# Row norms between the softmax sums, a reordered prologue, and keys, values and router norms moved ahead, in an eight-stage transformer kernel on one core

## The chip, the cores and the metric

The kernel runs on one core of a Trainium2 chip. The core has five engines with a queue of instructions each: TensorE (PE, with its weight loads shown as PEld), VectorE (DVE), ScalarE (ACT), GpSimd (POOL) and SyncE (SP, which here only issues transfers). They meet only through semaphores. The metric is the time of one execution on the device in microseconds (us); lower is better.

## The reference, cut to what matters

The input x is 16 batches of 128 tokens of width 128; the context is 16 x 77 tokens of the same width. Four layers follow, each with an attention-like part and an FFN-like part, and each part is added to x with the tanh of a gate:

```
x = x + tanh(g_xattn[0]) * L0_xattn(layernorm(x), ctx, ctx, mask)  # 16 heads of 64, masked, softmax
x = x + tanh(g_ffn[0])   * L0_ffn(layernorm(x))     # switch MoE, 8 experts, capacity S/E
x = x + tanh(g_xattn[1]) * L1_xattn(layernorm(x), ctx)  # linear mix, plus the mean of ctx
x = x + tanh(g_ffn[1])   * L1_ffn(layernorm(x))     # SwiGLU, fake-quantised by global maxima
x = x + tanh(g_xattn[2]) * L2_xattn(layernorm(x), ctx, ctx)  # one head of 128
x = x + tanh(g_ffn[2])   * L2_ffn(layernorm(x))     # top 2 of 8 experts, and 2 shared ones
x = x + tanh(g_xattn[3]) * L3_xattn(layernorm(x), ctx)  # self and context attention, 16 heads of 8
x = x + tanh(g_ffn[3])   * L3_ffn(layernorm(x))     # expert choice over tokens
```

`layernorm` is (x - mean) / sqrt(var + eps) over the 128 features, without weights. In `L0_xattn` q = x wq + bq and k = ctx wk + bk. In `L2_ffn` the gates are a softmax over the two highest router logits of each token.

## The kernel before

x stays on the chip as tile `X` [128 tokens, 16 batches, 128]. Each stage has one function for each engine (`tensor_attn0`, `vector_attn0`, `scalar_attn0`, `gpsimd_attn0` and so on), and each engine runs the stages one after the other, in the order in which the code is written. So the order of work in a queue is the order by hand; `wait_ge(semaphore, n)` holds an engine until another has counted up to n. `linked` and `pooled` make an engine wait for its own last result. A float32 product is run by PE in two passes, so that the trace counts two for each instruction. Timeline rows join neighbours of one line, as x4.

**First attention** (`*_attn0`, 0 to about 250 us). In the prologue wq and wk are multiplied into a key weight per head (`G0`; L622), and wq with bk into `beta` (L628: 16 products, each of 64 rows, since two heads share the 128 partitions), wv and wo into a value weight (`wvo0`; L645), and bv and wo into a bias row (L649, L650). DVE and ACT copy them out of the PSUM banks, `prep0_*` being the semaphores. Then comes a loop over the 16 batches. For each one PE makes keys (L516) from ctx and `G0`, scores (L546 adds the mask, L547 multiplies), transposes of the exponentials (L559), values (L525, L534) and the output (L591). DVE takes maxima (L723, L727), subtracts (L732), sums the exponentials in three pieces (`sums`, L738, each after ACT's exponential of that piece, L901), and inverts the sums (L741); POOL multiplies by them (L1006). Rows of batch b+2 are normalised in turn b: DVE's `stats` (L706, L708), POOL's rstd (L990, L991), DVE's `apply` (L713, tile `xn`), PE's transpose (L575), ACT's copy (L906). DVE also normalises rows for the first router within the loop.

**First MoE and linear mix** (250 to 345 us). Tokens go to experts by indirect transfers through memory and come back the same way (`y_tokens`); DVE adds the returned ones to X (L1301). The mix (`tensor_mix1`) has a product that spreads per-batch rows (L1273), six warming products on ones (`keep_busy`, L445), and then for four groups of four batches: transposes (L1253), ACT's copy, product.

**Quantised FFN** (345 to 385 us). At its end DVE has, for each of four groups, an output scaling and an addition to X (L1443, L1445).

**Third attention** (`*_attn2`, 385 to 427 us). First keys and values of all 16 batches (L1478: three products, L1482: sixteen), copied by ACT (L1562) and DVE (L1524, with the bias) into `kT2` and `v2` in area A of the on-chip memory. Then four groups: the norm of the rows in DVE (`vector_g_stats`, L1229, L1232; `vector_g_apply`, L1246) and POOL (L1237, L1238), transposes (L1253), queries (L1493), scores (L1498), maximum and subtraction (L1531, L1533), exponential (L1573), transposes (L1511), product with values (L1517), scaling and addition (L1555, L1557).

**Second top-2 MoE** (`*_moe2`, 427 to about 540 us). For each of the four groups: statistics, rstd and rows, transposes into bank `GT2`, ACT's copy into `xnT2` (L1747), logits (L1609). Then DVE's `route` (L1684 to L1700): top two, differences, an exponential by ACT (L1751), gates, and their split into bfloat16 parts (L1697 to L1700). PE meanwhile does `up(0)` and `up(1)` (L1616) and the context keys and values of the fourth attention (`tensor_aux3`: L1831, L1835; ACT L2049, L2053). POOL's `gpsimd_aux3` (L2119 to L2122) splits these keys into bfloat16 parts, which SP sends on (`sync_aux3`). Then PE transposes the gates (L1622), and pairs of experts run: `up` (L1616), ACT's Silu (L1743), DVE's products (L1712, L1714). ACT loads a table of functions when it goes from Exp to Silu or back (ACT_TABLE_LOAD rows).

## Time and profile before

| | |
|---|---|
| median of three runs | 797.06 us |
| the runs | 792.36, 797.06, 799.18 us |
| the profiled execution | 798.87 us, span 796.5 us |
| mean granted clock of TensorE | 0.884 |
| PE busy | 629.6 us (79%) |
| DVE busy | 455.9 us (57%) |
| ACT busy | 325.3 us (41%) |
| POOL busy | 216.0 us (27%) |
| busy PE, 46 to 250 us | 189.22 of 204 us |
| busy PE, 385 to 430 and 430 to 475 us | 32.47 of 45 and 35.34 of 45 us |

The span is what the profiler recorded from the first to the last instruction; the time of the execution has a little more around it. The granted clock is the share of full speed that the throttle let TensorE have; its levels are 2.4 GHz (1.00) and 1.2 GHz. A row of the timeline has start, duration, engine, line, operation, output<-inputs, shapes; in brackets how long the engine was idle before it and what released it. Engines work side by side, so only the one that others wait for sets the time.

### The profile page before, as it was taken

How to read it: one execution, taken by the hardware profiler on the slowest of the kernel's cores; microseconds unless marked ns; L12 is line 12 of the kernel's file. 1: busy time of each engine (PE TensorE's matmuls, PEld its weight loads, DVE VectorE, ACT ScalarE, POOL GpSimd, SP SyncE). 2: the span in 40 equal slices, each digit the busy share in tenths (PEclk: the TensorE clock that was granted, in tenths of full speed). 3: DMA queues.
4: the chain of work that ended last, by engine and by line, in shares of the span. 5: the costliest groups of instructions: out<-in, count | busy, mean ns of one | idle time of the engine just before them, and what ended most of it. 6: DMA issues, size and time to landing. Idle time of an engine off the chain costs nothing.

```text
span 796.5 us, 14168 instructions
## 1 busy us (share of the span) xinstructions
PE 629.6 (79%) x5413; PEld 420.5 (53%) x5413; DVE 455.9 (57%) x1244; ACT 325.3 (41%) x700; POOL 216.0 (27%) x407
## 2 busy tenths in 40 slices
PE   3889999999988596553685879989888878857687
PEld 3656565666656384421454525554555555534674
DVE  2266576676767412779666455536666666165362
ACT  1354435353433241534231422313676676512154
POOL 2032323334253446400112212421252511020210
PEclk9999999999999698656797779999899999755789
DMA  7840000000000253000000040203020300020001
GB/s 241 226 163 1 1 1 1 1 7 8 1 9 19 90 159 112 0 0 1 1 0 1 0 109 15 78 7 103 5 77 21 91 7 6 3 107 0 2 0 54
DMA packets 33604, 34.50 MB, mean 43 GB/s; under 512 B 8730, under 2 KB 29506, under 8 KB 32962
## 3 DMA queue, kind: packets, MB, share of 16 engines
q1 hardware_dynamic: 31072, 31.02, 13.4%
q0 software_dynamic: 1024, 2.11, 0.8%
q8 instruction: 44, 0.72, 0.4%
q10 hardware_dynamic: 1442, 0.48, 0.3%
q14 instruction: 22, 0.18, 0.1%
HBM read 19.62 MB, written 5.26 MB: 31 GB/s over the span
## 4 chain that ended last, share of the span: by engine, by line
PE 51%; DVE 18%; issue 12%; ACT 11%; POOL 4%; DMA 1%; POOLq 0%; DVEq 0%; ACTq 0%; SPq 0%
PE bank L1616 5%; PE bank L1859 5%; PE bank L591 4%; PE bank L547 4%; PE bank L1874 3%; ACT area_a L927 3%; PE bank L1661 3%; PE bank L1907 2%; ACT area_a L901 2%; PE bank L525 2%; PE bank L2287 2%; PE bank L534 2%; POOL y_tokens L1197 2%; DVE mx L2010 2%; ACT area_a L920 2%
## 5 line engine op out<-in xcount | busy, mean ns | idle before, releaser
L2010 DVE TENSOR_REDUCE mx<-bank 128x4 f32<-128x512 f32 (+1 forms) x128 | 71.0, 581 | 39.7 <-PE bank L1867 39.3
L2078 ACT ACTIVATE area_a<-bank 128x512 f32<-128x512 f32 (+1 forms) x128 | 73.7, 597 | 39.2 <-PE bank L1874 37.8
L927 ACT ACTIVATE area_a<-bank,beta 128x154 f32<-128x154 f32 x128 | 42.0, 413 | 85.9 <-PE bank L516 85.8
L591 PEld LDWEIGHTS bank<-area_a 128*128 128x128 f32 x384 | 46.7, 191 | 24.7 <-issue 24.7
L1006 POOL TENSOR_TENSOR area_a<-area_a,rs 128x512 f32<-128x512 f32 (+1 forms) x48 | 40.9, 879 | 60.6 <-DVE rs L741 60.6
L591 PE MATMUL bank<-area_a 128*128 128x128 f32 x384 | 53.5, 283 | 0.0
L746 DVE COPY area_a<-bank 128x512 f32<-128x512 f32 x32 | 22.1, 689 | 42.1 <-PE bank L525 21.1
L1237 POOL TENSOR_TENSOR g_veps<-g_mv,eps 128x4 f32<-128x4 f32 x20 | 4.0, 201 | 152.5 <-DVE g_mv L1232 152.5
L1616 PE MATMUL bank<-area_a 128*128 128x512 f32 x80 | 43.1, 668 | 0.2 <-DVE area_a L1714 0.2
L516 PE MATMUL bank<-ctx_flat,area_a 128*128 128x154 f32 x256 | 41.4, 296 | 2.3 <-ACT area_a L927 2.2
L516 PEld LDWEIGHTS bank<-ctx_flat,area_a 128*128 128x128 f32 x256 | 36.3, 190 | 10.3 <-issue 7.1
L547 PE MATMUL bank<-area_a,xnT 128*128 128x512 f32 (+1 forms) x96 | 41.6, 515 | 0.0
L1253 PE MATMUL bank<-ident,xn 128*128 128x128 f32 x80 | 17.8, 364 | 26.2 <-DVE xn L1246 15.8
L525 PE MATMUL bank<-area_a,ctx_flat 128*64 128x512 f32 x128 | 34.3, 617 | 0.1
L920 ACT ACTIVATE area_a<-bank 128x512 f32<-128x512 f32 x48 | 29.9, 624 | 8.7 <-PE bank L559 8.7
L445 PE MATMUL bank<-ones_b 128*128 128x512 bf16 x84 | 25.8, 415 | 7.6 <-DVE drow L1102 5.3
L990 POOL TENSOR_TENSOR ln_veps<-ln_mv,eps 128x1 f32<-128x1 f32 x32 | 6.3, 196 | 92.2 <-DVE ln_mv L708 90.8
L901 ACT ACTIVATE area_a<-area_a 128x512 f32<-128x512 f32 (+1 forms) x48 | 28.3, 590 | 6.6 <-DVE area_a L732 6.6
L2159 POOL CAST mcol<-mx 128x16 bf16<-128x16 f32 x32 | 5.3, 196 | 93.3 <-DVE mx L2010 93.3
L559 PE MATMUL bank<-ident,area_a 128*128 128x128 f32 x192 | 29.2, 277 | 1.7 <-ACT area_a L920 1.7
L559 PEld LDWEIGHTS bank<-ident,area_a 128*128 128x128 f32 x192 | 22.3, 141 | 15.1 <-issue 15.1
L1874 PE MATMUL bank<-area_a,area_b 64*77 64x128 bf16 x256 | 23.3, 231 | 8.6 <-ACT area_a L2078 8.0
(360 smaller groups left out, 1513.8 us busy)
## 6 DMA issues: line engine op xcount, KB each, us to landing
area_a<-xn_area SPq DMA_DIRECT2D x48, 128.0 KB, 2.7
area_b<-in_w SPq DMA_DIRECT2D x16, 256.0 KB, 4.9
f<-in_f SPq DMA_DIRECT2D x1, 2048.0 KB
area_a<-in_f SPq DMA_DIRECT2D x1, 2048.0 KB, 7.9
area_b<-xn_area SPq DMA_DIRECT2D x6, 308.0 KB, 5.6
area_a<-in_rows SPq DMA_DIRECT2D x10, 128.0 KB, 2.7
x_slots<-xn_area SPq DMA_DIRECT2D x1, 1032.0 KB, 7.4
area_a<-x_slots SPq DMA_DIRECT2D x8, 129.0 KB, 2.4
```

The source lines that it names most:

```text
L516: m = pe.matmul(dst[:, (h - lo) * 2 * T:(h - lo + 1) * 2 * T], G0[:, h, :], ctx_flat[:, 2 * g * T:(2 * g + 2) * T], start=True, stop=True)
L525: m = pe.matmul(dst[64 * r:64 * r + 64, :], ctx_flat[:, b * T:b * T + 64], wvo0[:, 8 * n + r:8 * n + 8:2, :], start=True, stop=True)
L547: pe.matmul(S0[c][:, 0:n * w], xnT[:, b % 2, :], kk0[:, b // 2 % 2, lo:hi, (b % 2) * T + t0:(b % 2) * T + t1], start=False, stop=True).the ...
L559: m = pe.transpose(T0[c % 2][:, i * 128:(i + 1) * 128], flat(part), ident[:, :])
L591: m = pe.matmul(WO, eT0[:, i, :], vv0[:, b % 2, i, :], start=(i == 0), stop=(i == 11))
L901: act.activation(probs0(b, c), probs0(b, c), ACT.Exp, scale=DK0 ** -0.5).then_inc(exp_done, 1)
L920: act.activation(flat(eT0[:, 4 * c:4 * c + 4, :]), T0[c % 2][:, :], ACT.Copy).then_inc(turn_done, 1)
L927: m = act.activation(kk0[:, g % 2, h, :], src[:, (h - lo) * 2 * T:(h - lo + 1) * 2 * T], ACT.Identity, bias=beta0[:, h:h + 1])
L1616: m = pe.matmul(SETS2[n % 2][a][:, :], w13_2[:, a, PAIRS2[n % 5], :], xnT2[:, n // 5, :], start=True, stop=True)
L1874: return pe.matmul(EXP_RING3[j % 2][0:n, i * 128:(i + 1) * 128], keys3(b, aux, p, ROWS3, c), queries3(b, p, ROWS3, c), start=True, stop=True)
L2010: dve.tensor_reduce(mx3[:, b % 2, aux, heads3(half, 1 - odd)], SCORES_RING3[j % 2][:, 0:4 * n].rearrange("p (h k) -> p h k", k=n), AX.X, A ...
L2078: act.activation((ea3 if aux else em3)[:, heads3(half, odd), :], EXP_RING3[j % 2][0:T if aux else 128, :].rearrange("p (h q) -> p h q", q= ...
```

## The change

1. In the loop of the first attention, `apply(b + 2)` (new line L720) goes from behind the reciprocal to between the first and the second of the three sums.
2. In the prologue, `bk0` is laid out as blocks [128, 8, 2], so that beta takes eight products of 128 rows. PE's order becomes: key weights, beta, transposes, keys 0 and 1, first value product, keys 2 to 5, scores, keys 6, second value product, keys 7, bias row, keys 8. DVE and ACT follow it. ident and ones are counted with the first rows of x; spare_slot goes behind the mask and ident_b in ACT's queue; POOL converts the mask behind the two rstd; the tanh goes behind the keys.
3. Keys and values of the third attention (`tensor_keys2` and its partners) go ahead of the mix; `kT2` and `v2` lie in area B. The six warming products go.
4. At the end of the quantised FFN, DVE does the statistics of all four groups of the third attention's norm, and the rows of the first two, between and behind its outputs.
5. In the third attention's loop, DVE and POOL do the router's norm for each group, and PE transposes groups 0 and 1 and makes their logits. Groups 2 and 3 follow in the second MoE.
6. In the second MoE, PE does `up(0)`, `up(1)` and two pieces of the fourth attention's context keys ahead of groups 2 and 3. ACT does keys, copies, two pieces of values, the exponential, the rest of the values and then the first Silu. POOL's split waits for the gates (`gates2_done`), and SP's transfers of constants for the end of the third attention.

```diff
-        bk0 = sb("bk0", [128, 8])
+        bk0 = sb("bk0", [128, 8, 2])
...
-        kT2 = carve("A", (at2, (B, T,)), 128)
-        v2 = carve("A", (at2, (B, D,)), T)
+        at2b = [0]
+        kT2 = carve("B", (at2b, (B, T,)), 128)
+        v2 = carve("B", (at2b, (B, D,)), T)
...
-                for r in range(2):
-                    p = slice(64 * r, 64 * r + 64)
-                    m = pe.matmul(bank[4 + r][:, j:j + 1], wq0[p, j, :], bk0[p, j:j + 1], start=True, stop=True)
+                m = pe.matmul(bank[4][:, 2 * j:2 * j + 2], wq0[:, j, :], bk0[:, j, :], start=True, stop=True)
             m.then_inc(prep0_in_psum, 1)
-            pe.wait_ge(const_loaded, 5 * 16)
+            pe.wait_ge(x_first, 3 * 16)
             for b in range(2):
                 pe.wait_ge(xn_done, b + 1)
                 pe.transpose(bank[6][:, b * 128:(b + 1) * 128], xn[:, b, :], ident[:, :]).then_inc(xnT_in_psum, 1)
-            pe.wait_ge(wvo0_loaded, 4 * 16)
...
-            pe.wait_ge(const_loaded, 5 * 16)
+            pe.wait_ge(x_first, 3 * 16)
...
+            pe.wait_ge(ctx_loaded, 16)
+            pe.wait_ge(prep0_act_done, 2)
+            pe.wait_ge(prep0_dve_done, 2)
+            keys(0)
+            keys(1)
+            value_weights(0)
+            for n in range(2, 6):
+                keys(n)
+            pe.wait_ge(prep0_dve_done, 4)
+            pe.wait_ge(pool_ready, 3)
+            pe.wait_ge(const_loaded, 3 * 16)
+            scores(0)
+            keys(6)
+            value_weights(1)
+            keys(7)
             for j in range(8):
                 pe.matmul(bank[7][0:1, 0:D], bv0[:, j:j + 1], wo0[:, j, :], start=(j == 0), stop=False)
             pe.matmul(bank[7][0:1, 0:D], ones_row[:, 0:1], bo0[:, :], start=False, stop=True).then_inc(prep0_in_psum, 1)
-            pe.wait_ge(ctx_loaded, 16)
-            pe.wait_ge(prep0_act_done, 2)
-            pe.wait_ge(prep0_dve_done, 4)
-            for n in range(6):
-                keys(n)
-            pe.wait_ge(pool_ready, 3)
-            scores(0)
-            for n in range(6, 9):
-                keys(n)
+            keys(8)
...
-            def sums(b):
+            def sums(b, norm=None):
+
                 u = b % 2
                 for c, (lo, hi) in enumerate(HEADS0):
+                    if c == 1 and norm is not None:
+                        apply(norm)
                     dve.wait_ge(exp_done, 3 * b + c + 1)
                     m = dve.tensor_reduce((slong0[:, lo:hi], slong0[:, lo:hi], sshort0[:, :])[c], probs0(b, c), AX.X, ALU.add)
...
+            key_weights(0)
             apply(0)
             apply(1)
-            dve.wait_ge(const_loaded, 5 * 16)
+            key_weights(1)
+            dve.wait_ge(prep0_in_psum, 3)
+            dve.tensor_copy(beta0[:, :], bank[4][:, 0:H0]).then_inc(prep0_dve_done, 2)
+            value_weights(0)
+            dve.wait_ge(const_loaded, 3 * 16)
             dve.wait_ge(pool_ready, 2)
             dve.tensor_copy(row_ids, spare_slot[:, :]).then_inc(ids_written, 1)
-            for half in range(2):
-                dve.wait_ge(prep0_in_psum, half + 1)
-                dve.tensor_copy(G0[:, 8 * half + 1:8 * half + 8:2, :], bank[2 * half + 1][:, :].rearrange("p (j d) -> p j d", d=D)).then_inc(prep0_dve_done, 1)
-            dve.wait_ge(prep0_in_psum, 3)
-            dve.tensor_copy(beta0[:, 0:H0:2], bank[4][:, 0:8])
-            dve.tensor_copy(beta0[:, 1:H0:2], bank[5][:, 0:8]).then_inc(prep0_dve_done, 2)
-            for half in range(2):
-                dve.wait_ge(prep0_in_psum, half + 4)
-                dve.tensor_copy(wvo0[:, 8 * half + 1:8 * half + 8:2, :], bank[5][:, :].rearrange("p (j d) -> p j d", d=D)).then_inc(prep0_dve_done, 1)
+            softmax(0)
+            value_weights(1)
+            sums(0)
...
-                    sums(j)
-                if b + 2 < B:
-                    apply(b + 2)
+                    sums(j, b + 2 if b + 2 < B else None)
...
+        def tensor_keys2(pe):
+            pe.wait_ge(late_loaded, LATE_LOADS * 16)
+            for n, (lo, hi) in enumerate(KB2):
+                if n == 2:
+                    pe.wait_ge(y_done, E0 - 1)
+                pe.matmul(KV2[n][:, 0:(hi - lo) * T], wqkv2[:, 1, :], ctxT[:, lo:hi, :].rearrange("p b t -> p (b t)"),
+                          start=True, stop=True).then_inc(kv2_in_psum, 1)
+            pe.wait_ge(y_done, E0)
+            for n in range(4):
+                at_least(pe, k2_done, n)
+                for j in range(4):
+                    m = pe.matmul(KV2[3 + n][0:T, j * D:(j + 1) * D], ctxT[:, 4 * n + j, :], wqkv2[:, 2, :], start=True, stop=True)
+                m.then_inc(kv2_in_psum, 1)
...
-            pe.wait_ge(y_done, E0)
+            tensor_keys2(pe)
             pe.wait_ge(mix16_done, 2)
             for g in range(4):
                 pe.matmul(MIX[g][:, :], ones[0:B, :], mix_rows[:, 4 * g:4 * g + 4, :].rearrange("p b d -> p (b d)"), start=True, stop=False)
-            keep_busy(pe, XT4[0], 6)
+            pe.wait_ge(v2_done, 3)
             tensor_g_xnT(pe, 0, XT4[0])
             for g in range(4):
+                if g == 0:
+                    pe.wait_ge(v2_done, 4)
...
+            vector_values2(dve)
...
+                if g < 2:
+                    vector_g_stats(dve, g, 8 + g, 3 * B + 4 * g + 4)
+                if g in (1, 2):
+                    vector_g_apply(dve, g - 1, 3 + g, 7 + g)
+            for g in range(2, 4):
+                vector_g_stats(dve, g, 8 + g, 3 * B + 4 * g + 4)
...
+            keep_busy(pe, bank[7], 6)
             tensor_g_xnT(pe, 4, XT4[0])
-            pe.wait_ge(v2_done, 4)
-            pe.wait_ge(k2_done, 3)
-            keep_busy(pe, AV2, 8)
+            pe.wait_ge(x_updated, 3 * B + 12)
+            keep_busy(pe, S2[0], 2)
...
+                else:
+                    tensor_g_xnT(pe, g + 6, GT2)
...
+                if g == 2:
+                    pe.wait_ge(moe2_loaded, 5 * 16)
+                if g >= 2:
+                    tensor_logits2(pe, g - 2)
...
+                if g >= 1:
+                    vector_g_stats(dve, g - 1, g + 11, 4 * B + 4 * g)
                 dve.wait_ge(av2_in_psum, g + 1)
                 out = tmp512[:, g % 2, :].rearrange("p (j d) -> p j d", d=D)
                 linked(dve, dve.tensor_tensor(out, AV2[:, :].rearrange("p (j d) -> p j d", d=D),
                                        s2["out"][:, :].unsqueeze(2).to_broadcast([128, 4, D]), ALU.mult))
                 dve.tensor_tensor(X[:, 4 * g:4 * g + 4, :], out, X[:, 4 * g:4 * g + 4, :], ALU.add).then_inc(x_updated, 4)
+                if g == 3:
+                    vector_g_stats(dve, 3, 15, 5 * B)
+                if g >= 1:
+                    vector_g_apply(dve, g - 1, g + 7, g + 11)
+            vector_g_apply(dve, 3, 11, 15)
...
-            for k in range(8, 12):
+            for k in range(8, 16):
...
-            tensor_aux3(pe)
+            pe.wait_ge(late_loaded, LATE_LOADS * 16)
+            pe.wait_ge(ahead_step, 7)
+            tensor_keys3(pe, 0)
+            tensor_keys3(pe, 1)
+            for g in range(2, 4):
+                tensor_g_xnT(pe, g + 8, GT2)
+                tensor_logits2(pe, g)
+            tensor_keys3(pe, 2)
+            for n in range(4):
+                tensor_values3(pe, n)
...
+            scalar_keys3(act, 0)
+            scalar_keys3(act, 1)
+            scalar_g_xnT2(act, 2)
+            scalar_g_xnT2(act, 3)
+            scalar_keys3(act, 2)
+            act.wait_ge(pool3_done, 1)
+            scalar_values3(act, 0)
+            scalar_values3(act, 1)
+            act.wait_ge(gap2_done, 1)
+            act.activation(r2s["e"][:, :], r2s["d"][:, :], ACT.Exp).then_inc(gap2_done, 1)
+            scalar_values3(act, 2)
+            scalar_values3(act, 3)
             silu(0, 0)
             silu(0, 1)
-            act.wait_ge(gap2_done, 1)
-            act.activation(r2s["e"][:, :], r2s["d"][:, :], ACT.Exp).then_inc(gap2_done, 1)
-            scalar_aux3(act)
...
-            for k in range(12, 16):
-                gpsimd_g_rstd(pool, k)
+            pool.wait_ge(gates2_done, 1)
             gpsimd_aux3(pool)
...
+            sp.wait_ge(x_updated, 5 * B)
...
+            act.dma_start(ident[:, :], t["ident"]).then_inc(x_first, 16)
+            act.dma_start(ones[:, :], t["ones"]).then_inc(x_first, 16)
             act.dma_start(mask_u8[:, :, :], t["mask"]).then_inc(mask_loaded, 16)
             act.dma_start(ident_b[:, :], t["ident_b"]).then_inc(const_loaded, 16)
+            act.dma_start(spare_slot[:, :], t["spare_slot"]).then_inc(const_loaded, 16)
```

PE in the prologue, before; area_a holds the weights, and L645 is the value product:

```order
L622 MATMUL bank<-area_a 128x128 x16
L628 MATMUL bank<-bk,area_a 128x1 x16
L633 MATMUL bank<-ident,xn 128x128 x2
L645 MATMUL bank<-area_a 128x128 x16
L649 MATMUL bank<-area_a,bv 1x128 x8
L650 MATMUL bank<-bo,ones 1x128
L516 MATMUL bank<-ctx_flat,area_a 128x154 x16
L546 MATMUL bank<-mask_bias,ident_b 128x208
```

And in the changed kernel:

```order
L638 MATMUL bank<-area_a 128x128 x16
L642 MATMUL bank<-bk,area_a 128x2 x8
L647 MATMUL bank<-ident,xn 128x128 x2
L517 MATMUL bank<-ctx_flat,area_a 128x154 x6
L628 MATMUL bank<-area_a 128x128 x8
L517 MATMUL bank<-ctx_flat,area_a 128x154 x10
L547 MATMUL bank<-mask_bias,ident_b 128x208
L517 MATMUL bank<-ctx_flat,area_a 128x154 x3
L628 MATMUL bank<-area_a 128x128 x8
```

The value product (now L628) stands between pieces of keys (L517), and the bias row (L649, L650 before) is behind the first scores.

DVE in the first full turn of the loop, before, with `xn` the rows of batch b+2:

```order
L706 BN_STATS ln_stats<-X 128x6
L708 BN_AGGR ln_mv<-ln_stats 128x2
L738 TENSOR_REDUCE slong<-area_a 128x8 x2
L738 TENSOR_REDUCE sshort<-area_a 128x16
L740 TENSOR_TENSOR sum<-slong,sshort 128x16
L741 RECIPROCAL rs<-sum 128x16
L713 TENSOR_SCALAR xn<-X,ln_mv,ln_rstd 128x128
L746 COPY area_a<-bank 128x512 x2
```

In the changed kernel:

```order
L713 BN_STATS ln_stats<-X 128x6
L715 BN_AGGR ln_mv<-ln_stats 128x2
L748 TENSOR_REDUCE slong<-area_a 128x8
L720 TENSOR_SCALAR xn<-X,ln_mv,ln_rstd 128x128
L748 TENSOR_REDUCE slong<-area_a 128x8
L748 TENSOR_REDUCE sshort<-area_a 128x16
L750 TENSOR_TENSOR sum<-slong,sshort 128x16
L751 RECIPROCAL rs<-sum 128x16
L756 COPY area_a<-bank 128x512 x2
```

The row of `xn` has moved up past two sums, the addition of the sums and the reciprocal.

PE at the start of the second MoE, before. The first two rows are the fourth of four such pairs of transposes and logits, L1616 is `up`, L1831 and L1835 are context keys and values:

```order
L1253 MATMUL bank<-ident,xn 128x128 x4
L1609 MATMUL bank<-rw,area_a 128x8 x4
L1616 MATMUL bank<-area_a 128x512 x4
L1831 MATMUL bank<-ctx_flat,wqk 128x512 x2
L1831 MATMUL bank<-ctx_flat,wqk 128x208
L1835 MATMUL bank<-wv,ctx_flat 77x128 x16
```

In the changed kernel, from the last product of the third attention (L1590) on; L1545 are logits, L1676 is `up`:

```order
L1590 MATMUL bank<-area_b,area_a 128x128 x4
L1545 MATMUL bank<-rw,area_a 128x8 x4
L1676 MATMUL bank<-area_a 128x512 x4
L1897 MATMUL bank<-ctx_flat,wqk 128x512 x2
L1280 MATMUL bank<-ident,xn 128x128 x4
L1545 MATMUL bank<-rw,area_a 128x8 x4
L1280 MATMUL bank<-ident,xn 128x128 x4
L1545 MATMUL bank<-rw,area_a 128x8 x4
L1897 MATMUL bank<-ctx_flat,wqk 128x208
L1902 MATMUL bank<-wv,ctx_flat 77x128 x16
```

Two of the pairs are gone from here into the third attention, one of their logits at the head of this piece, and the other two stand behind `up` and two pieces of keys.

## Rows read from the trace of the kernel before

**Rows 1.** Windows: us, PE, PEld, DVE, ACT, POOL busy, PEclk, DMA.

```profile
100.00:150.00 50.00, 47.16 (x300) 31.93 (x300) 35.94 (x103) 22.38 (x63) 14.86 (x28) 1.00 0.00 1
400.00:450.00 50.00, 38.03 (x181) 25.82 (x180) 28.35 (x108) 13.58 (x23) 7.23 (x12) 0.80 0.00 0
```

**Rows 2.** One line's instructions, L575: xcount, min/median/max ns, first to last start, shape.

```profile
L575 PE MATMUL bank<-ident,xn x14: 301/329/331, 55.2 to 234.3; 128*128 128x128 f32 x14
```

**Rows 3.** Who waited for L713: releaser's waiter, us, times.

```profile
  PE bank L575: 14.5, 14
```

**Rows 4.** Timeline, one loop turn: start, duration, engine, line, operation [idle before <-releaser].

```profile
65.69 0.55 POOL L991 TENSOR_TENSOR ln_rstd<-ln_veps,minus_half 128x1 f32<-128x1 f32 x1
...
66.95 0.69 DVE L738 TENSOR_REDUCE slong<-area_a 128x8 f32<-128x512 f32 x1 [0.32 <-ACT area_a L901]
...
68.50 0.26 DVE L713 TENSOR_SCALAR xn<-X,ln_mv,ln_rstd 128x128 f32<-128x128 f32 x1
...
68.82 0.33 PE L575 MATMUL bank<-ident,xn 128*128 128x128 f32 x1 [0.96 <-DVE xn L713]
```

**Rows 5.** Timeline of PE, prologue.

```profile
12.66 3.44 PE L628 MATMUL bank<-bk,area_a 64*128 64x1 f32 x32
...
23.09 2.08 PE L645 MATMUL bank<-area_a 64*128 64x128 f32 x16 [0.87 <-DVE area_a L836]
25.10 3.44 PE L649 MATMUL bank<-area_a,bv 128*1 128x128 f32 x16
...
28.77 1.84 PE L516 MATMUL bank<-ctx_flat,area_a 128*128 128x154 f32 x12
...
35.49 0.26 PE L546 MATMUL bank<-mask_bias,ident_b 128*128 128x208 bf16 x1 [0.85 <-ACT area_a L927]
...
45.72 0.27 PE L546 MATMUL bank<-mask_bias,ident_b 128*128 128x208 bf16 x1
```

**Rows 6.** DMA issues: tiles, queue, xcount, KB each, us to landing.

```profile
ones<-in_ones ACTq DMA_DIRECT2D x1, 64.0 KB, 9.3
```

**Rows 7.** Timeline, ahead of the linear mix.

```profile
306.95 3.70 PE L1273 MATMUL bank<-area_a,ones 16*128 16x512 f32 x8 [0.52 <-DVE area_b L1170]
...
314.10 1.14 DVE L1301 SCALAR_TENSOR_TENSOR X<-xn_area,r_weight,X 128x128 f32<-128x128 f32 x4 [7.20 <-DMA xn_area<-y_tokens]
```

**Rows 8.** Timeline, head of the third attention.

```profile
385.35 4.45 PE L1478 MATMUL bank<-ctx_flat,wqkv 128*128 128x462 f32 x6 [3.27 <-DVE X L1445]
...
389.58 3.91 PE L1482 MATMUL bank<-wqkv,ctx_flat 128*77 128x128 f32 x32
...
402.45 0.48 DVE L1531 TENSOR_REDUCE s_max<-bank 128x4 f32<-128x308 f32 x1 [2.31 <-PE bank L1498]
```

**Rows 9.** Timeline, from the third attention's end to the route.

```profile
425.50 0.69 DVE L1557 TENSOR_TENSOR X<-tmp,X 128x512 f32<-128x512 f32 x1
...
428.79 1.12 DVE L1246 TENSOR_SCALAR xn<-X,g_mv,g_rstd 128x128 f32<-128x128 f32 x4 [0.23 <-POOL g_rstd L1238]
429.00 1.01 POOL L1238 TENSOR_TENSOR g_rstd<-g_veps,minus_half 128x4 f32<-128x4 f32 x1
...
444.38 0.29 DVE L1684 TENSOR_TENSOR area_a<-bank,rb 128x128 f32<-128x128 f32 x1 [8.39 <-PE bank L1609]
```

**Rows 10.** Timeline, gates of the second MoE.

```profile
444.19 5.62 PE L1616 MATMUL bank<-area_a 128*128 128x512 f32 x8
...
452.00 0.17 DVE L1691 TENSOR_SCALAR r2s_den<-r2s_e 128x16 f32<-128x16 f32 x1 [3.57 <-ACT r2s_e L1751]
...
454.80 2.52 POOL L2120 TENSOR_TENSOR area_a<-area_a,xn_area 128x1232 f32<-128x1232 f32 x1
454.84 2.63 DVE L1698 TENSOR_TENSOR area_a<-area_a 128x128 f32<-128x128 f32 x1
...
461.48 0.59 PE L1622 MATMUL bank<-ident_b,area_a 128*24 128x128 bf16 x4 [5.16 <-DVE area_a L1700]
...
470.52 1.98 PE L1616 MATMUL bank<-area_a 128*128 128x512 f32 x4 [0.19 <-DVE area_a L1714]
```

185 lines of the change are left out of this document (86 added, 99 removed).

## The prediction

> **What bounds the kernel now.** I read the profile from coarse to fine: the busy table, the sums over windows, who waits for which line, and the timeline of the places that the diff touches. The profiled execution has a span of 796.5 us and a time of 798.87; the sum is made against the 798.87. It lies 1.8 above the median of 797.06, so a sum against the median would read 1.8 lower.
>
> In the busy table PE stands well ahead of DVE, the next engine. In the first attention's loop PE works for 47.16 of 50 us and its granted clock is 1.00; around the third attention it works for 38.03 of 50 us and the mean granted clock is 0.80, part of the time at the 1.2 GHz level [rows 1]. So three things can shorten the kernel: a gap of PE in the loop, the ramp ahead of the loop, and the chains of small steps between 385 and 470 us, where PE is idle or slow. The change touches all three. A gap of another engine is worth nothing here.
>
> **Part 1: the row normalisation between the sums (the loop of the first attention).** In each turn PE transposes the new rows (L575), and these come from DVE's L713, which stands behind the reciprocal. There are 14 such transposes between 55.2 and 234.3 us, thus a turn is (234.3-55.2)/13 = 13.78 us [rows 2]. PE waits for L713 in all 14, 14.5 us together, 1.04 each [rows 3]. Its new place is L720, behind the first of the three sums. In the turn at 65 us, POOL has the rstd at 65.69+0.55 = 66.24. DVE ends the first sum at 66.95-0.32 = 66.63, then idles 0.32 until ACT has the second exponential. L713 starts only at 68.50, and PE, free since 68.82-0.96 = 67.86, starts at 68.82 [rows 4]. In the new order L713 (0.26) runs from 66.64 to 66.90, in the idle 0.32 of DVE, so the second sum isn't late, and xn is there 0.9 before PE asks. The wait goes whole in this turn. What would be late next: the slack of 0.9 is larger than a jitter of tenths, but turns in which DVE also does router work are fuller. As an estimate I give 0.7 back over the loop. Bounds: nothing gained if another result (ACT's copy of an earlier transpose, POOL's product with the reciprocals) is just as late, 14.5 at most. I take **-13.8**, near the upper bound, because the row shows 0.9 of slack and DVE's own idle covers the 0.26.
>
> **Part 2: the prologue.** The 16 products for beta, each on 64 rows and run in two passes, take 3.44 us from 12.66 [rows 5]. Eight on 128 rows are 16 passes instead of 32, but each loads weights of twice the rows: between half of it (1.7) and all (3.4). I take 3.0, near the upper end, since the passes have one or two columns and the loads set the pace; so beta ends at 12.66+3.0 = 15.7. ident and ones now count as first loads, and DVE's statistics wait for them: ones takes 9.3 us from its issue [rows 6], the fifth of ACT's queue and under 3 us, thus about 12 (X itself lands about 3 us before). Then POOL's two rstd and DVE's two rows: transposes from 15.7 to about 17.0, just behind beta. Pieces 0 to 5 of the first keys took 35.49-28.77 = 6.7 us, with the value products (2.08 each) and the bias row (3.44 and a short last product, 3.7) all ahead of them [rows 5]. Now two pieces (1.8), one value product (2.08) and four pieces (3.7) follow the transposes: 17.0+7.6 = 24.6 for the first scores instead of 35.49, -10.9. Not all of this reaches the loop. From the first scores to the loop's own it is 45.72-35.49 = 10.2 us; the second value product (2.08) and the bias row (3.7) now stand in this stretch, +5.8, of which about 1.5 fills the wait that PE has there for ACT: 14.5. The loop starts at 24.6+14.5 = 39.1 instead of 45.72: **-6.5**. Bounds: -7.5 (all of the PE gaps filled) and -3 (ident, ones or the gates land 3 us later than now, since their order on ACT's queue changes). The mask's conversion on POOL moves behind the two rstd and the tanh behind the keys; both are needed only at the first scores and at the end of turn 0. Of the DMAs, SP's indirect writes wait for the ids that DVE now writes some 3 us later, and nothing of the first turn reads them.
>
> **Part 3: keys and values of the third attention ahead of the mix.** They cost PE 4.45+3.91 = 8.4 us from 385.35 [rows 8]. They now stand behind the last expert product. PE would have gone on at 306.95, and DVE waits for the returned tokens until 314.10, 7.2 us [rows 7]. The 8.4 were run at the low level (0.74 a pass of 462 columns); by the 0.495 and 0.70 of Part 5 the high level makes 5.9 of them. PE has just been busy with the experts, so I take 6.2, with the last values' addition by DVE at 313.6, just before 314.10. The mix rows (3.70) end at 316.5 and are needed first behind the transposes, for which PE idles anyway. The six warming products go, so the mix may start slow. I take **0**; bounds +2 (8.4 and 3.70 both at the low level push DVE past 314.10) and -1.5 (PE stays fast into the mix).
>
> In the tail of the quantised FFN, DVE does the statistics and rows of groups 0 and 1 between its output groups. The first maximum of the third attention stands at 402.45 [rows 8], 17.1 us behind 385.35. The keys and values (8.4) leave that path, along with DVE's statistics and row work of group 1; transposes, queries and scores, with waits, remain: first maximum near 394.2 at the low clock, 392.9 at the high. I take **-8.3**, bounds -9.5 and -5 (DVE's added work of some 5 us delays the last FFN group).
>
> **Part 4: router norms in the loop.** Before, the last addition of the attention ends at 425.50+0.69 = 426.2, and then four groups go one by one through statistics, rstd, rows (1.12), transpose and logits until the route starts at 444.38 [rows 9]. Now two groups are through in the loop, which costs PE two sets of transposes and logits, about 2.9 us. Last addition 426.2-8.3+2.9 = 420.8; then the two upward products (5.62, slow [rows 10]), two of the keys (2.2 to 2.8) and two rounds of transpose, copy and logits (4.4 to 5.5), the lower ends taken: 433.0 instead of 444.38, -11.4, thus **-3.1** beyond the -8.3. Bounds +1.5 and -5.
>
> **Part 5: the exponential and POOL's split.** DVE waits 3.57 until the exponential is done (452.00), since a Silu with its table stands ahead of it; with Exp first the wait shrinks to about 0.3: **-3.3**. From 452.00 to PE's next product at 461.48 DVE then has ten small operations (L1691 to L1700). L1698 takes 2.63 us while POOL's L2120 takes 2.52 from almost the same moment [rows 10]; the same size costs DVE 0.29 where POOL is still [rows 9]. At 0.17 to 0.3 each the first six are 1.6 of the 9.5 us, the last four 7.7 with starts and waits. POOL now waits for the gates, so the four become 1.2: **-6.5**. PE then multiplies at 0.495 a pass (1.98/4) instead of 5.62/8 = 0.70 if it is fast [rows 10]; after the gates I assume the same mix of both. The split itself (some 7.5 us of POOL) ends later, relative to the rest; its result is sent to the fourth attention, far behind. Bounds of the part: -5 (the split then blocks DVE's products) and -11.
>
> First what the rows show on POOL and DVE together: beside the blocked L1698, L1246 took 1.12 for four while POOL's L1238 (1.01) ran from 429.00, and no longer than elsewhere [rows 9]. The Trainium skill (SBUF — State Buffer, "Who interferes with whom") says that DVE and GpSimd share a port pair under an exclusive lock and that a one-input DVE operation can also take it. By that rule the norms' rows, of which four sets now meet POOL's rstd, would lose up to 1 us each, and the time would be 4 us more; the rows of 428.79 and 429.00 do not bear this out.
>
> **The sum.** -6.5 -13.8 +0 -8.3 -3.1 -3.3 -6.5 = -41.5, and 798.87-41.5 = 757.4. Behind the gates PE is busy most of the time and shifts as a whole.
>
> **The rivals.**
> - *The loop's wait is replaced.* Another result ends last, 0.1 to 0.5 us after L713's new time. For it: DVE is busy 35.94 of 50 us in the loop [rows 1]. Against it: 0.9 of slack. With half the gain +7: 764; with none 771. Chance 0.13.
> - *The low clock or a late chain eats the router part.* More small steps with gaps between 395 and 440: if all passes of the attention and of the first products run at 0.70 instead of 0.495, some 35 passes lose 0.2 each, 7 us, and the loop of the third attention gets the norms on its DVE path, 3 more: 764 to 768. For it: 0.80 in the window [rows 1]. Chance 0.13.
> - *The norms' rows collide with POOL's rstd.* Four to six rows with 1.0 each (the length of L1238): 761 to 763. Chance 0.06.
> - *Slower.* One mechanism: without its gap of 1.04 a turn PE works for nearly all of the loop, and the granted clock falls there to the 1.2 GHz level. A pass then takes 0.70 instead of 0.495, 1.41 times; 12.8 us by 0.41 is 5.2 a turn, 84 for 16 turns. It decides from eight slow turns on (41.5/5.2); with all, 841. For it: only that full load is new. Against it: 1.00 at 47.16 of 50 [rows 1], the low levels stand where PE idles. Chance 0.02.
> - *It doesn't do what it says.* The dispatch of the ahead work stalls the mix and the moved transposes, and the gains of 20 us from parts 3 to 5 vanish: 778. Chance 0.02.
> - *Better.* PE stays fast from 385 to 470 and the prologue's gaps all close: below 750. Chance 0.06.
>
> **How the numbers follow.** My forecast, 757, has the chance 0.58, with 750 to 764 as its own range. The range goes to 770 for the cases of a lost half loop and a slow router part, and down to 748 for a part of the better case. A change of 1% (8 us) is about what a measurement tells from none. All cases but the slower one, and a sum of several losses, gain more than 1%: faster 0.96, same 0.02, slower 0.02.
>
> **What would show it.** Step by step in the changed trace: the first scores near 24.6 and the loop's near 39; the wait of PE for xn below 1 us in all; turns of 12.8; keys and values done by 314 with the addition of tokens still near its start; the first maximum 8 us nearer to the last FFN addition; DVE's four casts and products of the gates at about 0.3 each; POOL's split behind them. The prediction is wrong if turns stay above 13.3, if PE shows a new wait of some tenths per turn, or if the gates end less than 15 us earlier, relative to the loop's end.

## The result

The changed kernel took 748.99 us in the median of four executions (742.46 to 755.36), the kernel before 796.64 (792.36 to 799.18, now four). The ratio is 0.9331, interval 0.9261 to 0.9402, so 6.7% faster: 53 us by the ratio, against 41.5 predicted. By the ratio the time is 743.3, 4.7 below the low end of the range; the plain median is inside it. The two differ because the executions of the changed kernel fall into two groups, at 743 and at 754 us, and the ratio is taken over the first.

The profiled execution has 743.47 us (span 741.6), 55.4 less than 798.87. The page's busy table, for the changed kernel:

```profile
span 741.6 us, 14125 instructions
## 1 busy us (share of the span) xinstructions
PE 610.3 (82%) x5391; PEld 409.7 (55%) x5391; DVE 450.0 (61%) x1243; ACT 321.1 (43%) x698; POOL 216.0 (29%) x407
```

PE works 19.3 us less than before (629.6). Only 22 passes are gone (16 of beta, six warming ones), so most of these 19.3 us are no waiting that went, but passes that ran faster. Where the time went mark by mark, from the first or last start of marked lines in both traces (named by the lines of before; a share is what the difference changes since the mark above; differences and shares are taken from the unrounded starts):

| mark | before | changed | difference | part's share | predicted |
|---|---|---|---|---|---|
| first loop transpose L575 | 55.2 | 42.8 | -12.4 | -12.4 | -6.5 |
| last output product of the loop L591 | 256.0 | 230.1 | -25.8 | -13.4 | -13.8 |
| tokens added L1301 | 314.1 | 289.9 | -24.2 | +1.6 | 0 |
| first FFN output L1443 | 379.3 | 354.9 | -24.3 | -0.1 | 0 |
| first maximum L1531 | 402.4 | 368.3 | -34.2 | -9.8 | -8.3 |
| route L1684 | 444.4 | 407.6 | -36.8 | -2.6 | -3.1 |
| gates' first step L1691 | 452.0 | 412.6 | -39.4 | -2.6 | -3.3 |
| gates' transposes L1622 | 461.5 | 415.4 | -46.1 | -6.6 | -6.5 |
| last of the pairs L1714 | 528.0 | 482.8 | -45.1 | +0.9 | 0 |
| end of the fourth attention (last L1859 on area_a alone) | 693.5 | 646.5 | -47.0 | -1.9 | 0 |
| first L2287 of the last stage | 757.7 | 702.1 | -55.5 | -8.5 | 0 |

Windows of 50 us at the places of [rows 1] (us, then busy PE, PEld, DVE, ACT, POOL, granted clock, share of DMA, GB/s), changed kernel:

```profile
88.00:138.00 50.00, 50.00 (x326) 33.70 (x325) 37.64 (x115) 24.32 (x69) 17.82 (x32) 1.00 0.01 1
358.00:408.00 50.00, 42.35 (x202) 26.63 (x201) 33.58 (x124) 13.63 (x23) 9.51 (x16) 0.84 0.06 13
```

In the loop PE is busy for all 50 us where it was for 47.16; a turn is (206.8-42.8)/13 = 12.6 us long. The turn of [rows 4] reads as follows in the changed kernel's timeline:

```profile
53.24 0.55 POOL L1016 TENSOR_TENSOR ln_rstd<-ln_veps,minus_half 128x1 f32<-128x1 f32 x1
53.49 0.69 DVE L748 TENSOR_REDUCE slong<-area_a 128x8 f32<-128x512 f32 x1 [0.38 <-ACT area_a L917]
...
54.10 0.34 DVE L720 TENSOR_SCALAR xn<-X,ln_mv,ln_rstd 128x128 f32<-128x128 f32 x1
...
55.25 0.27 PE L576 MATMUL bank<-ident,xn 128*128 128x128 f32 x1
```

The rows are there at 54.44, PE asks at 55.25: 0.8 of slack. The list of waits from 42 to 208 us, in which all 14 transposes start, has one row left for this line (us in total, times, longest), against 14.5 us in [rows 3]:

```profile
PE bank L576 <- DVE xn L720: 0.7, 1, 0.7
```

The prologue on PE, to compare with [rows 5]:

```profile
9.53 3.79 PE L638 MATMUL bank<-area_a 64*128 64x128 f32 x32 [9.53 <-DVE area_a L829]
13.25 2.30 PE L642 MATMUL bank<-bk,area_a 128*128 128x2 f32 x16
...
17.50 1.16 PE L628 MATMUL bank<-area_a 64*128 64x128 f32 x16
...
22.88 0.26 PE L547 MATMUL bank<-mask_bias,ident_b 128*128 128x208 bf16 x1 [0.89 <-ACT area_a L943]
...
34.60 0.27 PE L547 MATMUL bank<-mask_bias,ident_b 128*128 128x208 bf16 x1
```

The same 16 passes of a value product took 2.08 before and take 1.16 now; nobody had changed them. And the gates, to compare with [rows 10]:

```profile
412.59 0.17 DVE L1760 TENSOR_SCALAR r2s_den<-r2s_e 128x16 f32<-128x16 f32 x1 [0.97 <-ACT r2s_e L1818]
...
414.41 0.29 DVE L1767 TENSOR_TENSOR area_a<-area_a 128x128 f32<-128x128 f32 x1
...
415.35 1.21 POOL L2186 CAST xn_area<-area_a 128x1232 bf16<-128x1232 f32 x1 [17.33 <-DVE area_a L1769]
415.43 0.38 PE L1682 MATMUL bank<-ident_b,area_a 128*24 128x128 bf16 x4 [1.04 <-DVE area_a L1769]
```

L1698's 2.63 us are L1767's 0.29, and POOL begins when DVE is through.

The steps of the sum, then, came out near their sizes, but four pieces are not in it: 5.9 in the prologue, 1.5 at keys and values, 1.9 in the fourth attention, and 8.5 in the last stages, where not a line was changed. The experiments ask two things: does each part do by itself what the sum says, and what made the rest? (Level stands below for the granted clock, low for 1.2 GHz.)

### The profile page after: what moved, and what is told of

The parts are those of the page before. It is cut to its first block, busy times and chain, and to the rows that moved or that the text cites. A ratio compares the mean times of both kernels' runs of the same rounds, so it can differ in the third digit from the quotient of the medians.

```text
span 741.6 us, 14125 instructions
## 1 busy us (share of the span) xinstructions
PE 610.3 (82%) x5391; PEld 409.7 (55%) x5391; DVE 450.0 (61%) x1243; ACT 321.1 (43%) x698; POOL 216.0 (29%) x407
## 4 chain that ended last, share of the span: by engine, by line
PE 62%; DVE 16%; issue 10%; ACT 4%; POOL 4%; DMA 3%; POOLq 0%; SPq 0%; DVEq 0%; ACTq 0%
PE bank L592 6%; PE bank L1676 6%; PE bank L1926 5%; PE bank L517 4%; PE bank L548 4%; PE bank L526 4%; PE bank L1941 3%; PE bank L1730 3%; PE bank L560 2%; PE bank L1974 2%; PE bank L2355 2%; PE bank L535 2%; DVE mx L2077 2%; POOL y_tokens L1224 2%; PE bank L446 2%
## 5 line engine op out<-in xcount | busy, mean ns | idle before, releaser
L592 PEld LDWEIGHTS bank<-area_a 128*128 128x128 f32 x384 | 48.2, 196 | 24.7 <-issue 15.0
L592 PE MATMUL bank<-area_a 128*128 128x128 f32 x384 | 55.0, 288 | 0.0
L1676 PE MATMUL bank<-area_a 128*128 128x512 f32 x80 | 42.8, 663 | 0.9 <-DVE X L1624 0.9
L517 PE MATMUL bank<-ctx_flat,area_a 128*128 128x154 f32 x256 | 41.6, 296 | 0.0
L517 PEld LDWEIGHTS bank<-ctx_flat,area_a 128*128 128x128 f32 x256 | 36.4, 190 | 7.9 <-issue 7.1
L446 PE MATMUL bank<-ones_b 128*128 128x512 bf16 x78 | 26.2, 443 | 6.6 <-DVE drow L1129 5.3
L560 PEld LDWEIGHTS bank<-ident,area_a 128*128 128x128 f32 x192 | 22.3, 142 | 15.1 <-issue 15.1
## 6 DMA issues: line engine op xcount, KB each, us to landing
area_b<-in_w SPq DMA_DIRECT2D x16, 256.0 KB
```

Of the source, the lines that this page charges most:

```text
L446: pe.matmul(psum[:, 0:n], ones_b[:, :], ones_b[:, :].unsqueeze(1).to_broadcast([128, n // 128, 128]), start=True, stop=True)
L517: m = pe.matmul(dst[:, (h - lo) * 2 * T:(h - lo + 1) * 2 * T], G0[:, h, :], ctx_flat[:, 2 * g * T:(2 * g + 2) * T], start=True, stop=True)
L560: m = pe.transpose(T0[c % 2][:, i * 128:(i + 1) * 128], flat(part), ident[:, :])
L592: m = pe.matmul(WO, eT0[:, i, :], vv0[:, b % 2, i, :], start=(i == 0), stop=(i == 11))
L1676: m = pe.matmul(SETS2[n % 2][a][:, :], w13_2[:, a, PAIRS2[n % 5], :], xnT2[:, n // 5, :], start=True, stop=True)
```

## The experiments

### The three parts alone

One kernel is the kernel before with this edit only:

```diff
-            def sums(b):
+            def sums(b, norm=None):
                 for c, (lo, hi) in enumerate(HEADS0):
+                    if c == 1 and norm is not None:
+                        apply(norm)
...
-                    sums(j)
-                if b + 2 < B:
-                    apply(b + 2)
+                    sums(j, b + 2 if b + 2 < B else None)
```

> The kernel before with part 1 alone: DVE normalises the rows of batch b+2 between the first two sums of the loop. Theory A (the transposes of PE were the only late ones and the rest of the turn holds): all 14 waits go, a turn falls from 13.78 to about 12.6 us, the loop is 14 to 15 us shorter, and the prologue and all that stands behind 260 us keep their durations; time about 783. Rival B (the gain in the loop needs the new prologue too, since the two meet in the first turns): less than 12 us. Rival C (the fuller loop drops the clock later): the loop gains 14 to 15, but stretches behind 260 us take longer than before.

The second has the prologue's part of the diff alone, the third all that stands behind the first attention.

> The kernel before with part 2 alone: the reordered prologue with the eight 128-row products for beta. Theory A (the prologue's gain is its own): the loop's scores start at 34.6 as in the changed kernel instead of 45.7, 11.1 us earlier, with the passes of the value products at about 272 ns against 417; time about 785.5. Rival B (the order of the loop fed back on it): a start later than 36.

> The kernel before with parts 3 to 6 alone (keys and values of the third attention ahead of the mix, norms in the tail and in the loop, the second MoE's order, POOL's split behind the gates). Theory A (parts add up): from the first output of the quantised FFN to the end of the second MoE's pairs it is 20 to 21 us shorter, nothing before, the mix within 0.3; the last two stages as they come by the clock; time about 776. Rival B (the 8.5 us of the last stages come from this part): the fourth attention and the last stage are 8 us shorter here as well, with their clock above that of the kernel before, time about 768.

| | median, us | ratio to before, interval | where it shows in the trace |
|---|---|---|---|
| norms alone | 778.94 | 0.9721 (0.9623 to 0.9819) | L575's first to the loop's last product 185.7 us instead of 200.8 |
| prologue alone | 787.89 | 0.9840 (0.9763 to 0.9917) | first loop transpose at 47.4 instead of 55.2 |
| rest alone | 776.14 | 0.9712 (0.9628 to 0.9797) | first FFN output to gates' transposes 60.5 us instead of 82.2 |

The norms give 15.1 us in the loop, somewhat more than the wait itself (14.5): theory A. The rest alone gives 21.7 us on its stretch against a forecast of 8.3+3.1+3.3+6.5 = 21.2: theory A for the parts. The prologue alone refutes its theory A: at the first transpose it brings 7.8 us, not the 12.4 of the changed kernel's profile, near the forecast of 6.5. At the loop's last product 4.5 of them are left (251.5 against 256.0). The turns up to the last are as long as before; then the window from 226 to 230 us reads a granted clock of 0.58, where the kernel before reads 1.00. The end of this kernel says less than its marks: at L2287 its profile is 11.6 us ahead, and 8.2 of these lie behind the fourth attention, where nothing was changed. Its trace says why the start is later than in the changed kernel. PE of the prologue alone:

```profile
9.17 3.79 PE L637 MATMUL bank<-area_a 64*128 64x128 f32 x32 [9.17 <-DVE area_a L825]
12.88 3.57 PE L641 MATMUL bank<-bk,area_a 128*128 128x2 f32 x16
...
19.99 2.02 PE L627 MATMUL bank<-area_a 64*128 64x128 f32 x16
...
26.24 0.26 PE L546 MATMUL bank<-mask_bias,ident_b 128*128 128x208 bf16 x1 [0.89 <-ACT area_a L941]
```

It is the same code as the changed kernel's prologue, but beta took 3.57 instead of 2.30 and the value product 2.02 instead of 1.16; only from about 22 us on are the passes fast. So TensorE's first products ran slowly here, by a factor of 1.5 to 1.8, and the moment at which that ends differs between executions.

### Does the form of beta decide it?

The changed kernel with beta by 64 rows:

```diff
-                m = pe.matmul(bank[4][:, 2 * j:2 * j + 2], wq0[:, j, :], bk0[:, j, :], start=True, stop=True)
+                for r in range(2):
+                    p = slice(64 * r, 64 * r + 64)
+                    m = pe.matmul(bank[(4, 7)[r]][:, j:j + 1], wq0[p, j, :], bk0[p, j, r:r + 1], start=True, stop=True)
```

> The changed kernel with beta again in 16 products of 64 rows with one column (two banks, two copies), all else as changed. Theory A (what TensorE does before the value products sets at which level they run): the beta passes take 330 ns loads and 3.4 us in all, and the passes of the next lines stay at the slow durations (417 instead of 272 ns in the first value product) for a while, so that the loop starts 1.5 to 4 us later than at 34.6. Rival B (only the beta products themselves count): they cost 1.1 us more and the value products run at 272 ns; the loop starts at about 35.7.

Beta took 3.44, the first value product 2.08, and the first scores stood at 26.2 against 22.9 (median 751.16, ratio 0.9392, interval 0.9298 to 0.9486). Alone that would have been a case for theory A. It isn't, since the prologue alone, with eight products of 128 rows, had the same slow passes and its first scores at 26.2 too. In slow passes the new form gains nothing, 3.57 against 3.44: the pass count halves, and each pass takes twice as long. My 3.0 fits neither level; beta took 3.57 in slow passes and 2.30 where they became fast on the way. What the old form costs in fast passes no run shows.

### POOL's wait and the exponential's place

```diff
         def gpsimd_moe2(pool):
-            pool.wait_ge(gates2_done, 1)
             gpsimd_aux3(pool)
```

> The changed kernel without POOL's wait for the gates: POOL splits the context keys as soon as they are there, as in the kernel before. Theory A (the four DVE operations L1766 to L1769 were slow because POOL ran beside them): the two of 128x128 that now take 0.3 us take over 1 or 2.6 us again, and from the route's start to the gates' transposes it is 5 to 7 us longer than the 7.8 us of the changed kernel; the pairs after it shift with it; time 4 to 6 us above the changed kernel's. Rival B (it was the exponential's place alone): within 1 us of 7.8.

The timeline of this kernel within the route:

```profile
412.36 1.21 POOL L2185 CAST xn_area<-area_a 128x1232 bf16<-128x1232 f32 x1 [11.75 <-ACT area_a L2115]
412.59 1.13 DVE L1749 TENSOR_TENSOR area_a<-area_a,r2s_r 128x128 f32<-128x128 f32 x1
...
413.65 2.52 POOL L2186 TENSOR_TENSOR area_a<-area_a,xn_area 128x1232 f32<-128x1232 f32 x1
413.75 2.57 DVE L1755 SCALAR_TENSOR_TENSOR area_a<-area_a 128x128 f32<-128x128 f32 x1
...
416.24 1.21 POOL L2187 CAST xn_area<-area_a 128x1232 bf16<-128x1232 f32 x1
416.36 0.29 DVE L1745 TENSOR_REDUCE r2s_m<-area_a 128x16 f32<-128x128 f32 x1
...
423.15 0.29 DVE L1767 TENSOR_TENSOR area_a<-area_a 128x128 f32<-128x128 f32 x1
```

From the route's start (410.97) to the gates' transposes (424.17) it is 13.2 us instead of 7.9, +5.3: theory A by the size, though at another place than I had said. The split now comes so early that it meets the route's operations, and L1767 is as quick as ever. So what is slow is not one particular line, but an operation on two tiles beside a wide one of POOL: 0.29 becomes 1.13 beside the cast and 2.57 beside the subtraction, each nearly the length of POOL's own row. It isn't everything that DVE does, either: the reduction L1745 at 416.36 keeps its 0.29 beside a cast of 1.21. The Trainium skill (SBUF — State Buffer, "Who interferes with whom") describes a port pair that DVE and GpSimd lock in turn; the rows agree for these operations.

The norms' rows can be slowed too, but not by POOL's rstd. In the changed kernel's first profile, behind the gates, four of them stand beside wide operations of POOL:

```profile
458.48 1.15 POOL L2187 TENSOR_TENSOR tmp<-tmp,xn_area 128x512 f32<-128x512 f32 x1
458.92 3.93 DVE L1273 TENSOR_SCALAR xn<-X,g_mv,g_rstd 128x128 f32<-128x128 f32 x4
460.39 1.16 POOL L2189 TENSOR_TENSOR xn_area<-tmp,xn_area 128x512 bf16<-128x512 f32 x1
```

They take 3.93 us instead of the 1.09 to 1.12 of other places, some of which have POOL's rstd of 128x4 beside them. The kernel before has the same 3.93 at 504.06, so the change neither made nor mended this one.

The whole kernel without POOL's wait lost more than 5.3 us (median 770.45, four executions between 759.5 and 776.9). The profile has 176 us between the last pair and the end of the fourth attention, where the changed kernel has 164 and 166, with the same waits of PE as in the kernel of the next experiment (168 us) and more of it at the low level. So only the 5.3 of the stretch are shown to come from the split.

The exponential, with the first two Silu ahead of it again:

```diff
+            silu(0, 0)
+            silu(0, 1)
             scalar_keys3(act, 0)
...
             scalar_values3(act, 3)
-            silu(0, 0)
-            silu(0, 1)
```

> The changed kernel with ACT's first two Silu ahead of everything in the second MoE, as before, so that a table is loaded to Silu, to Exp and to Silu again. Theory A: the two Silu and two table loads (1.28 each) stand ahead of the exponential, DVE's wait for it grows by 2 to 3 us, the gates come 2 to 3 us later; time 2 to 3 us above the changed kernel's. Rival B (the exponential isn't what the gates wait for): no change within 0.5 us.

```profile
413.54 1.28 ACT L1820 ACT_TABLE_LOAD   x1
414.83 0.22 ACT L1820 ACTIVATE r2s_e<-r2s_d 128x16 f32<-128x16 f32 x1
...
415.08 0.17 DVE L1760 TENSOR_SCALAR r2s_den<-r2s_e 128x16 f32<-128x16 f32 x1 [2.40 <-ACT r2s_e L1820]
```

DVE waits 2.40 instead of 0.97, and route to transposes takes 9.3 instead of 7.9: +1.4, less than the 2 to 3 expected. The two Silu themselves hide in a wait of ACT (4.98 and 1.90 us idle before them); the table load (1.28) covers most of the 1.4. Median 753.54, ratio 0.9458 (0.9398 to 0.9519).

### Keys and values back

The changed kernel, with `tensor_keys2` and its partners called at the head of the third attention instead of ahead of the mix, the mix's warming products back, and without the six that the change put ahead of the third attention:

> The changed kernel with the third attention's keys and values back at that attention's head, behind the whole FFN, and the six warming products back in the mix; the norms stay where the change put them. Theory A (the 8.4 us of keys and values were the path there): from the first FFN output to the first maximum it is 21 to 23 us as in the kernel before (23.1) instead of 13.4; the mix keeps its time; 8 us slower than e9. Rival B (the norms moved into the FFN's tail bring most of it): 15 to 17 us.

From the first FFN output to the first maximum it was 23.9 us, in the changed kernel 13.3, before 23.2. So without the move of keys and values nothing of this gain is left: theory A. Median 762.39, ratio 0.9546 (0.9494 to 0.9598). Where PE begins the keys, this kernel's timeline reads

```profile
364.41 4.19 PE L1298 MATMUL bank<-ctx_flat,wqkv 128*128 128x462 f32 x6 [7.82 <-DVE X L1501]
```

That is 10.6 us behind the first FFN output, where it was 6.1 before: the norms in the FFN's tail hold up DVE's additions to X, and PE idles 7.82 for them instead of 3.27 [rows 8]. From the keys to the first maximum it is then 13.3 instead of 17.1. The norms cost 4.6 on one side of the keys and give back 3.8 on the other, so with the keys in their old place they bring nothing. Whether the keys' move alone, with the norms in their old place, would bring all of the 9.8 us was not run.

Rows of the changed kernel show what they cost in their new place:

```profile
281.92 2.24 PE L1298 MATMUL bank<-ctx_flat,wqkv 128*128 128x462 f32 x6
283.99 3.66 PE L1304 MATMUL bank<-wqkv,ctx_flat 128*77 128x128 f32 x32
...
289.89 1.14 DVE L1359 SCALAR_TENSOR_TENSOR X<-xn_area,r_weight,X 128x128 f32<-128x128 f32 x4 [1.52 <-DMA xn_area<-y_tokens]
```

5.9 us instead of 8.4 of [rows 8], behind busy experts, and DVE still idles 1.52 for the transfer: free, as forecast.

### What the last stages and the prologue owe to the clock

In the kernel before, TensorE's granted clock is 0.50 from 690 to 740 us, though PE works for 33.91 of these 50:

```profile
690.00:740.00 50.00, 33.91 (x254) 21.92 (x254) 23.95 (x76) 12.21 (x24) 4.78 (x8) 0.50 0.12 42
```

The waits of PE are nearly those of the changed kernel: of before (693 to 745 us) and of the changed one (646 to 702 us) the list of waits begins

```profile
PE bank L1253 <- DVE xn L1246: 7.1, 3, 4.5
PE bank L2267 <- ACT area_b L2382: 2.7, 4, 0.7
PE bank L2250 <- ACT xnT L1258: 2.7, 4, 0.7
```

```profile
PE bank L1280 <- DVE xn L1273: 7.1, 3, 4.5
PE bank L2335 <- ACT area_b L2450: 3.2, 4, 1.1
PE bank L2318 <- ACT xnT L1285: 2.7, 4, 0.7
```

Over the whole stretch from the fourth attention's end to L2287, PE is busy for 41.56 us before (mean clock 0.58) and for 32.60 in the changed kernel (0.80). So it is the passes, not the waits, that took 8.5 us less. The kernels with one part each have 63.5 (norms), 56.0 (prologue) and 58.9 us (rest) there, though none of them changes a line of it. If this is a level that any kernel can have there, keeping PE busy should lift it:

```diff
+            keep_busy(pe, bank[5], 10)
             logits(0)
             logits(1)
             for g in range(4):
+                keep_busy(pe, bank[5], 1)
                 pe.wait_ge(perm3_done, g + 1)
...
                 m.then_inc(pt3_in_psum, 1)
+                keep_busy(pe, bank[5], 1)
                 pe.wait_ge(pt3_done, g + 1)
...
                 if g < 2:
+                    keep_busy(pe, bank[5], 3)
                     logits(g + 2)
+                elif g == 3:
+                    keep_busy(pe, bank[5], 3)
```

> The changed kernel with 10 + 2x3 + 3 + 8 products on ones between the waits of PE at the start of the last stage. Theory A (the 8.5 us that the last stages gained beyond the parts are the level of TensorE's clock, which differs between executions of the same code): with PE kept busy the stretch from the stage's first transposes to the products L2355 is at the high level in most executions, 1 to 4 us shorter than in the changed kernel's profile and 6 to 10 shorter than in the kernel before; the executions of this kernel lie within 6 us of each other. Rival B (the gain there was from the change itself, for instance transfers that no longer collide): no difference, or a loss of the added 5 us.

The median was 743.72 (739.45 to 744.40), ratio 0.9308 (0.9261 to 0.9355), the stretch from L1859's last to L2287's first 54.3 us. The changed kernel and this one were then run together on one chip:

> The changed kernel once more, for the spread of its executions beside e10 and e11 on one chip. Theory A (the same code falls into different clock levels in the prologue and behind the fourth attention): its profile shows another duration of the prologue (the loop starts between 34.6 and 38) and of the stretch from the last product of the fourth attention to the products L2355 (55 to 64 us) than the first profile's 34.6 and 55.6, with all else within 1.5 us; executions spread over 10 us or more. Rival B (the change fixed these levels): 34.6 and 55.6 again, executions within 3 us.

> The kernel of e8 once more, beside the changed kernel on one chip. Theory A (busy TensorE holds the level in the last stage): the stretch to L2355 is 54 to 56 us again, the executions spread less than those of e9, and the median is 4 to 8 us below that of e9. Rival B (e8 had luck): the same median as e9 within 2 us.

The changed kernel: 742.1, 743.1, 753.3, 753.9, 754.7 and one at 792.2, median 753.62. With the fillings: six between 740.2 and 746.3, median 743.60, ratio to before 0.9318 (0.9275 to 0.9361), stretch 51.8. The changed kernel's profile was again from the group at 743, with 55.5 in the stretch but its loop's first transpose at 45.4 instead of 42.8. So the first profile was lucky in its prologue, by 2.7 us against this one; in nine traces that share this prologue's code the loop's scores start between 34.6 and 38.1, and the first profile has the earliest. Theory A holds there as well. But the luck didn't last: at the loop's last product the two profiles are 1.0 apart (230.1 and 231.2), since in the first one the end of the loop ran partly at the low level, and at the tokens none of it is left (289.9 and 289.3). And the same fillings in the kernel before:

> The kernel before with the fillings of e8 in the last stage and nothing else. Theory A (the 8.5 us that the sum of the parts doesn't hold are a level of TensorE's clock that has nothing to do with the change): the stretch from the last product of the fourth attention to the products L2287 falls from 64.2 to 52 to 56 us here too, the median by 5 to 9 us, to about 791. Rival B (the change itself made this stretch faster): it stays at 60 to 64, the median within 2 us of the kernel before.

Median 789.48 (788.74 to 792.96) against 799.56, ratio 0.9885 (0.9857 to 0.9914); the stretch fell from 64.2 to 54.2 us with all marks up to 693.5 as before. Theory A: the stretch can be as short without the change, if PE is kept busy. With the fillings in both kernels the whole change brings 45.9 us (789.48 and 743.60, medians of six executions each, on two chips; 45 by their ratios to the kernel before). Two single executions of the changed kernel caught both groups:

> The changed kernel, one look for the stretch to L2355 in a slower execution. Theory A: an execution of about 754 us has 62 to 64 us there, one of about 743 has 55 to 56, and the marks up to the fourth attention's end are within 2 us of each other. Rival B: the 11 us between the two groups of executions lie somewhere else, or are spread over all stages.

> As e14, another look: theory A 62 to 64 us at about 754 and 55 to 56 at about 743; rival B a difference in other stages.

The first took 744.55, the second 754.69. Their marks lie within 0.6 us up to the last pair (484.1 and 483.9), then 1.8 apart at the end of the fourth attention, and 10.3 at L2355. The same window in the two, the one of 744.55 first:

```profile
646.00:686.00 40.00, 24.26 (x254) 15.44 (x254) 23.33 (x75) 11.32 (x22) 4.79 (x8) 0.74 0.15 53
```

```profile
646.00:686.00 40.00, 25.99 (x181) 16.48 (x182) 19.92 (x70) 9.35 (x18) 4.78 (x8) 0.50 0.15 53
```

In the second the level is 1.2 GHz throughout, in the first 2.4 GHz for about half of it, although PE's waits in the stretch are the same. Of the 10.1 us between the two, 8.5 lie in this stretch: the same code has either level. What no run shows is that the kernel before, without fillings, has the high one too. Of 12 executions of the changed kernel five took 742.1 to 744.6 us; of 40 of the kernel before none took less than 792.3, and with the fillings it takes 789. So the change may well have made the high level more frequent there; how, stays open.

### Filling the prologue too

Twenty, then 32 products on a zeroed tile ahead of the first weights, the second with ten more ahead of the experts and with the fillings of the last stage:

```diff
+            pe.wait_ge(pool_ready, 1)
+            for _ in range(20):
+                pe.matmul(bank[7][:, :], warm0, warm0.unsqueeze(1).to_broadcast([128, 4, 128]), start=True, stop=True)
             pe.wait_ge(wqk0_loaded, 4 * 16)
```

> The changed kernel with 20 products on a zeroed tile in PE's queue ahead of the first weights' arrival, from about 1 us on. Theory A (TensorE runs its first products slowly, whatever their form, until it has worked for some time, and the moment of the rise decides the prologue): key weights take about 2.2 instead of 3.8 us, beta 2.3, all passes of the prologue are at the fast durations in every trace, the loop starts at 32.5 to 33.5 instead of 34.6 (lucky) or 38 (as in the prologue alone); time 2 to 4 us below the changed kernel's median. Rival B (the loads of the weights, or the transfers that run then, are slow): the same 3.8 and no gain.

```profile
0.99 5.88 PE L635 MATMUL bank<-tmp 128*128 128x512 bf16 x20 [0.99 <-POOL tmp L2539]
9.20 2.47 PE L642 MATMUL bank<-area_a 64*128 64x128 f32 x32 [2.32 <-DVE area_a L833]
11.60 3.57 PE L646 MATMUL bank<-bk,area_a 128*128 128x2 f32 x16
```

The key weights did take 2.47 instead of 3.79, though the transfers ran on beside them: the slow start is the clock, and rival B falls. But PE had stood idle for 2.32 us before them, and beta was slow again. Here the clock column shows the fall: the window from 10.7 to 20.9 us reads 0.50, the ones before and behind it 1.00. The first scores came at 25.1, about 1 us ahead of the more usual 26.2; the median of 755.87 can't be told from the changed kernel's.

> The kernel of e8 with two more fillings: 32 products on a zeroed tile from 1 us until the weights' shift is done, and 10 on ones in the wait ahead of the first experts. Theory A: key weights and beta both at the fast durations (2.4 and 2.3 us), loop start 33 to 34.6; experts' first products fast, 1 us; median 3 to 5 us below e10. Rival B (the level falls again whatever fills the prologue, as in e7, where key weights took 2.47 and beta 3.57): loop start at 36 to 37, no gain over e10.

Here the fillings went on until 10.7, past the moment at which the weights were ready, and the next 32+16 passes were fast (beta in 1.95), but the first value product was slow once more (2.08). Loop start at 36.0, median 746.22 (742.38 to 748.19), 2.6 above the kernel with the last stage filled alone: rival B. Filling the prologue wasn't worth it. The best version that I ran is the changed kernel with the last stage filled.

## Why the prediction was right or wrong

- **The loop (-13.8).** Right in its mechanism: the wait goes but for 0.7, POOL's and ACT's results are in time, nothing replaces it. The norms alone give 15.1, the second profile of the changed kernel too, the first one 13.4, as in that execution the end of the loop ran partly at the low level (window 222 to 230 us at 0.79). The 0.7 held back for fuller turns were not needed, and the transposes themselves became shorter (0.27 against 0.33).
- **The prologue (-6.5).** At the first transpose the order is worth 7.8 by the prologue alone; that was sized well, with errors that cancel (beta saves nothing; the scores come at 26.2, not 24.6, yet the loop's start needs less after them). In the first profile it was 12.4 there, which is luck by up to 4.6. The step that failed is "beta ends at 12.66+3.0" and every price behind it: I took durations of passes from rows at 12 to 28 us as if they belonged to the operations, while they belonged to a clock level whose end moves between 13 and 28 us. The clock column showed 1.00 from the start in both traces and gave no warning; the transposes would have: L633's took 0.45 and 0.47 us each, L575's of the same 128x128 take 0.33 [rows 2].
- **Mix (0).** Right; DVE idles 1.52 instead of 7.20 in front of the tokens. From the loop's last product to the tokens it was 58.1 us before. Four traces of the changed kernel have 58.2 to 59.8, and the norms alone, which leave the keys in their old place, have 59.6. So the first profile's +1.6 isn't shown to come from the keys; what makes it is open.
- **Keys and values, first maximum (-8.3).** 9.8 in the profile, just past the upper bound of 9.5, and 10.6 by putting them back. I held 1.2 back for DVE's added work in the FFN's tail. That work does cost, 4.6 us where PE waits for X behind it, but in the changed kernel no keys stand there to be held up; DVE idles 0.40 for PE in front of the first maximum.
- **Router norms (-3.1), exponential (-3.3), POOL (-6.5).** 2.6, 2.6 and 6.6. The exponential's wait shrank to 0.97, not 0.3, since ACT has two pieces of values ahead of it that wait for PE. Together 11.9 against 12.9.
- **"Behind the gates PE is busy most of the time and shifts as a whole."** This is the step that failed most: it puts the stretch at nothing, and in the two profiles it is 8.5 us in the last stages and 1.9 in the fourth attention. The shift was rigid where the clock was the same (the pairs: +0.9). But the last stage has waits of up to 4.5 us on PE, and there an execution of the changed kernel can be at the low level almost throughout (64.0 us, 754.69 in all) or for less than half of the stretch (55.5 us, 744.55 in all). The fourth attention differs by 1.9 between these two executions as well. The profile of the kernel before had the low level, that of the changed one much of the high, so the difference of two profiles carries this as if it were a gain of the edit; whether the edit has a part in how often the high level comes is open. Without the 8.5 the profiles differ by 46.9; with the level lifted by fillings in both kernels the medians differ by 45.9. That is some 4 us more than the 41.5, about 1.3 each from the prologue and the loop, 1.5 to 2.3 from keys and values, less 1.0 from router and gates. So the sizes of the parts were forecast well, that of the prologue partly by errors that cancel; what put the result outside the range was the term left at nothing.
- **The rivals.** The loop's wait wasn't replaced. The low clock around the third attention didn't come (0.84 in the window against 0.80). The collision of the norms' rows with POOL's rstd did not show: the applies of the router took 1.09 to 1.12 for four, one of them (396.57) with POOL's rstd of 397.02 beside it, as in [rows 9]. "No longer than elsewhere" overlooked one place of the same trace, the 3.93 us at 504.06 beside POOL's wide operations: the rows can be held up, by those. PE with full load in the loop kept 1.00 from 42 to 222 us (178.99 busy of 180): the slower rival has no support. "Better" was nearest, and I gave it 0.06 with a wrong reason, the level between 385 and 470. The range was too narrow below: it had no term for the level in stages that the change leaves alone, which these executions show to be worth 8 to 10 us. The other group of executions of the changed kernel, at 754, is inside the range and near the forecast: a comparison by that group would have hidden the error.

## What to carry to other kernels

Before the sum is made, look for stretches where the granted clock is at its low level though PE works for two thirds of the time. Such a stretch can come out at another level in the next execution, and a profile shows one: put its size into the range, on both sides, even for code that isn't touched, and compare profiles mark by mark rather than by their ends. A row's duration is a price only together with the level at which it was measured; compare passes of one shape across the trace. And where one small operation of DVE takes as long as POOL's row beside it, moving POOL's work behind the chain gives back the added time (here 6.6 us).

## What the runs showed of the hardware

- The first products of this program ran slowly up to a moment that differs: about 14 us in one execution of the changed kernel, about 20 in another, about 22 with the prologue alone, about 28 in the kernel before. The profile's clock column reads 1.00 there all the same. The Trainium skill (TensorE: Matmul & The Clock Gate, "Part 1: The HAM clock gate") says that the number of slow first products varies between runs of one kernel; these traces agree. It calls the cost of the ramp less than 1% of a typical span; the spread of 3.5 us of 745 in the loop's start agrees. The 8 to 10 us of the last stage, over 1%, are not this ramp but a later fall of the level.
- With filling products among its waits the same stage was never at the long duration in the 10 timed executions of the filled changed kernel (739.5 to 746.3 us in all), nor in the six of the filled kernel before (788.7 to 793.0), as far as the times of executions without a profile tell. The three profiles among them have 54.3, 51.8 and 54.2 us.
- A normalisation of one batch (128x128) took 0.34 at its new place and 0.26 at its old one, in the norms alone as well (346 ns in the median of its 16). No POOL row runs beside it at 54.10; why it is longer stays open, and the slack of 0.8 hides it.
- One execution of the changed kernel took 792.2 us, with a mean clock of 0.786. It has no profile, and what happened is open.
- DVE beside POOL: operations of 128x128 on two tiles went from 0.29 to 1.13 (cast of 128x1232) and 2.57 us (subtraction of 128x1232), rows of the norms from 1.1 to 3.93 for four beside operations of 128x512, while a reduction kept 0.29 and the norms' rows 1.1 beside the rstd of 128x4.
